# A level-embedding transformer tower on one core: ternary weights transposed by DMA, scores in plain fp32

## The chip, the core and the metric

The kernel runs on one core of a Trainium2 chip. The metric is the device time of one execution in microseconds. The kernel is written by hand: each of the engines TensorE (PE), VectorE (DVE), ScalarE (ACT), GpSimd (POOL) and SyncE (SP) runs its own list of instructions in order, and semaphores say what each waits for.

## What is computed

A table of 32 level embeddings is the only input of the attention, so `x` (16 sequences of 128 tokens) is turned into bracket levels first; after that the tower works on levels and counts, not on tokens. Cut to what matters:

```
delta  = is_open(x) - is_close(x);  levels = scan(clip(level + delta, 0, 31))
h      = level_emb[levels] * 0.15
h     += attention(layernorm(h))        # 16 query heads, 4 kv heads of 16, D = 256
Wq1, Wq2 = clip(round(W / (mean|W| + 1e-5)), -1, 1)       # ternary, W1 1024x256, W2 256x1024
h     += relu(layernorm(h) @ Wq1.T + b1) @ Wq2.T + b2     # output 16 x 128 x 256, fp32
```

## The kernel before

All tokens of a sequence that are at one level have one row, so there are 16 sequences x 32 levels = 512 rows, in four groups `g` of 128 rows (four sequences each). The stages are:

- **Head.** Constants by iota and comparison, the level scan on DVE, normalised table, queries and keys (`queries`, `keys`, `values`). Queries and keys are split in a high and a low fp32r part (`query_hi`, `query_lo`, `key_hi`, `key_lo`), and `scores_t(g)` adds for each group two fp32r matmuls of 512 columns and a bf16 one that masks absent levels (lines 1153, 1154, 1158). `less_max` subtracts the maxima, `exps(g)` takes the exponential on ACT.
- **Middle.** `context`, `inverse_sums`/`normalise` (`rec`, `cn`), `context_t`, `out_proj`, then `add_table`, `row_stats`, `row_moments`, `variance_eps` on DVE, the root on POOL (`inverse_root`, line 445), the normalised rows `xn2`, their transposes `rows_t` and their split in `xhi` (ACT) and `xlo` (DVE).
- **Weights, beside the middle.** `magnitudes` sums |W| on ACT in four passes of 128x1024 (line 528). W1 becomes ternary on ACT (`rounded`, line 537, and `ternary`, line 542), W2 on DVE (`signs`, line 867, and `ternary`, line 882). PE transposes both with an identity, `weights_t(u)`, u = 0 to 7, four 128x128 blocks each (line 1240), and ACT copies each result from PSUM (`weights_out(u)`, lines 549 and 551) to `w1T` or `w2T`.
- **FFN.** `ffn1(h, j)`: half `h` of the rows, hidden chunk `j`, four matmuls of 256 columns into PSUM bank `pswt` (line 1258); `hidden` on ACT applies the ReLU (`hr`, and `hh` for some), `hidden_lo` on DVE makes the low part; `ffn2(j, g)`: two matmuls of 256 columns into `psmisc` (line 1273). The order of both is written out by hand. Two `pswt` banks mean that an `ffn1` can start only when ACT has read the one before the last.
- **Tail.** `final(g)`, `spread(g)` (rows to tokens by one-hot matmuls, lines 1295 to 1298), `result(g)` copies to SBUF, ACT the first two sequences of a group and DVE the other two, and stores of 256 KB go out per pair.

Dependences that the change touches: `ffn1(0, j)` waits for `a_wt`, the copies of W1; `ffn2(j, 0)` waits for those of W2. POOL does four roots, two scaled means (`mr2`, for `norm_rows(2)` and `norm_rows(3)`) and four `residual`s behind its `counted_values`. Warm matmuls on zeros (`warm_up`, `keep_warm`) fill PE's gaps.

Of the kernel before, what the change touches and what calls it, by code (L numbers as in the profile page):

```python
# [36 lines left out]
def level_tower(nc, x, emb, Wq, bq, Wk, bk, Wv, bv, Wo, bo, W1, b1, W2, b2, out):  # L37
# [20 lines left out]
    with ctx:  # L58
# [35 lines left out]
        ident1 = sb("ident1", [P, P], BF16)  # L94
        ident2 = sb("ident2", [P, P], BF16)
# [52 lines left out]

        pmx = sb("pmx", [P, 2, P])
# [57 lines left out]
        c_ident = sem("c_ident")  # L207
# [51 lines left out]
        v_khi = sem("v_khi")  # L259
        v_klo = sem("v_klo")  # L260
        a_qhi = sem("a_qhi")
        v_qlo = sem("v_qlo")
# [3 lines left out]
        p_s = sem("p_s")  # L266
        v_pmx = sem("v_pmx")
# [26 lines left out]
        v_sgn = sem("v_sgn")  # L294
        p_gam = [sem(f"p_gam{i}") for i in range(2)]
        v_thr = sem("v_thr")
        v_tern = sem("v_tern")
        p_wt = sem("p_wt")
        a_wt = sem("a_wt")
# [18 lines left out]

        SPREAD_IN_PARTS = (0, 1)
# [13 lines left out]
        w1_rows = W1.rearrange("(p j) d -> p j d", j=FC)  # L333
# [10 lines left out]
        def _(sp):  # L344
# [4 lines left out]
            sp.dma_start(bvr[:], bv.unsqueeze(0)).then_inc(d_bv, 16)  # L349
            sp.dma_start(bkc[:], bk.unsqueeze(0).unsqueeze(2).to_broadcast([2, KVD, 1])).then_inc(d_bk, 16)  # L350
# [24 lines left out]
        def _(pool):  # L375
# [99 lines left out]
            counted_values(3)  # L475
            inverse_root(0)
            inverse_root(1)
            inverse_root(2)
            inverse_root(3)
            scaled_mean(2)  # L480
            scaled_mean(3)
            residual(0)
            residual(1)
            residual(2)
# [3 lines left out]
        def _(act):  # L488
            act.dma_start(tok3[:], x.unsqueeze(0).to_broadcast([3, B, S])).then_inc(d_tok, 16)
            act.dma_start(bq2[:], bq.rearrange("(k a e d) -> a e k d", k=KV, a=2, e=2)).then_inc(d_bq, 16)  # L490

# [20 lines left out]
            def query_hi(i):  # L512
                act.wait_ge(p_q, 1)
                c = slice(64 * i, 64 * i + 64)
                nc.scalar.activation(qs[c, :].rearrange("p (a e l) -> p a e l", a=2, e=2)[:, :, i, :],
                                     psg[3][c, 0:2 * L].rearrange("p (a l) -> p a l", a=2), ACT.Copy).then_inc(a_qhi, 1)
# [9 lines left out]
            def magnitudes(w, i):  # L526
                act.wait_ge((d_w1, d_w2)[w][i], 16)
                nc.scalar.activation(aw[:, w, i * 1024:(i + 1) * 1024], halves(w, i), ACT.Abs,  # L528
                                     accum_out=asum[:, 2 * w + i:2 * w + i + 1]).then_inc(a_abs, 1)

            def rounded(q):
                act.wait_ge(a_abs, 2)
                act.wait_ge(v_inv, 1)
                act.wait_ge(c_magic, 2)
                c = slice(1024 * q, 1024 * q + 1024)
                src = w1[:].rearrange("p j d -> p (j d)")[:, c]
                nc.scalar.activation(aw[:, 0, c], src, ACT.Identity, bias=magic[:, 0:1], scale=inv[:, 0:1]).then_inc(a_rnd, 1)
# [521 lines left out]
        def _(pe):  # L1059
# [157 lines left out]
            def weights_t(u):  # L1217
                w, i = divmod(u, 4)
                if w == 0:
# [4 lines left out]
                    if u == 1:  # L1224
                        pe.wait_ge(v_thr, 1)
# [200 lines left out]
```

## Time and profile before

| | us |
|---|---|
| three runs | 55.86, 55.99, 53.93 (median 55.86) |
| profiled execution | 54.04 |
| its span, first to last instruction | 52.0 |
| PE busy in it | 45.6 (88%) |
| DVE, ACT, POOL busy | 38.0 (73%), 34.2 (66%), 15.7 (30%) |

The chain of work that ended last is 76% PE, 10% DVE, 3% POOL and 1% ACT. The largest shares of it are the ffn1 matmuls with 16% and the ffn2 matmuls with 15%. A plain fp32 matmul stands in the trace as two records. The time of an execution is about 2 us longer than its span. In a timeline a row starts with its start and its busy time, then engine, line, operation, tiles and number.

### The profile page before, as it was taken

How to read it: one execution, taken by the hardware profiler on the slowest of the kernel's cores; microseconds unless marked ns; L12 is line 12 of the kernel's file. 1: busy time of each engine (PE TensorE's matmuls, PEld its weight loads, DVE VectorE, ACT ScalarE, POOL GpSimd, SP SyncE). 2: the span in 40 equal slices, each digit the busy share in tenths (PEclk: the TensorE clock that was granted, in tenths of full speed). 3: DMA queues.
4: the chain of work that ended last, by engine and by line, in shares of the span. 5: the costliest groups of instructions: out<-in, count | busy, mean ns of one | idle time of the engine just before them, and what ended most of it. 6: DMA issues, size and time to landing. Idle time of an engine off the chain costs nothing.

```text
span 52.0 us, 1206 instructions
## 1 busy us (share of the span) xinstructions
PE 45.6 (88%) x394; PEld 36.3 (70%) x394; DVE 38.0 (73%) x141; ACT 34.2 (66%) x77; POOL 15.7 (30%) x37
## 2 busy tenths in 40 slices
PE   0999999999999799999999999999999999993000
PEld 0336469894758688768679999989999798860000
DVE  3558994698985289999999996269858889659100
ACT  0083231380799997989988999999967793509000
POOL 5689952000005950009200579970000000000000
PEclk9999999999999999999999999999999999999997
DMA  0183919999753100000000000000000005555893
GB/s 0 36 234 77 44 63 350 410 432 368 198 124 98 47 7 0 0 0 0 0 0 13 0 0 0 0 6 0 0 0 0 0 13 200 203 208 195 295 385 127
DMA packets 4658, 5.37 MB, mean 103 GB/s; under 512 B 1117, under 2 KB 4141, under 8 KB 4653
## 3 DMA queue, kind: packets, MB, share of 16 engines
q1 hardware_dynamic: 4312, 5.02, 31.2%
q10 hardware_dynamic: 341, 0.29, 1.6%
q8 instruction: 3, 0.05, 0.4%
q14 instruction: 2, 0.02, 0.1%
HBM read 3.21 MB, written 2.10 MB: 102 GB/s over the span
## 4 chain that ended last, share of the span: by engine, by line
PE 76%; DVE 10%; POOL 3%; issue 1%; ACT 1%; DVEq 1%
PE pswt L1258 16%; PE psmisc L1273 15%; PE psg L1067 8%; PE psg L1063 5%; PE psg L1194 4%; POOL rs L445 3%; PE psg L1240 3%; DVE aw L952 2%; PE psg L1106 2%; PE psg L1153 2%; PE psg L1203 2%; PE psg L1154 2%; PE psg L1158 2%; DVE cn L892 2%; DVE hq L906 2%; DVE st L910 2%
## 5 line engine op out<-in xcount | busy, mean ns | idle before, releaser
L587 ACT ACTIVATE hr<-pswt,b1c 128x256 f32<-128x256 f32 x16 | 7.6, 484 | 1.2 <-PE pswt L1258 0.9
L1273 PE MATMUL psmisc<-w2T,hh 128*128 128x256 f32 x32 | 8.2, 285 | 0.0
L1273 PE MATMUL psmisc<-w2T,hl 128*128 128x256 f32 x32 | 8.1, 281 | 0.0
L937 DVE TENSOR_TENSOR hl<-hr,hh 128x256 fp32r<-128x256 f32 x16 | 6.7, 435 | 1.2 <-ACT hh L589 0.9
L1258 PE MATMUL pswt<-xhi,w1T 128*128 128x256 f32 x32 | 7.0, 299 | 0.0
L1258 PE MATMUL pswt<-xlo,w1T 128*128 128x256 f32 x32 | 6.4, 280 | 0.0
L1273 PEld LDWEIGHTS psmisc<-w2T,hh 128*128 128x128 f32 x32 | 6.0, 189 | 0.1
L1273 PEld LDWEIGHTS psmisc<-w2T,hl 128*128 128x128 f32 x32 | 6.0, 189 | 0.0
L445 POOL TENSOR_TENSOR rs<-ve,mhalf 128x1 f32<-128x1 f32 x4 | 2.7, 686 | 9.1 <-DVE ve L918 9.1
L440 POOL TENSOR_TENSOR voc<-vo,cpos 128x272 f32<-128x272 f32 x4 | 2.7, 714 | 8.1 <-DVE cpos L858 8.1
L1258 PEld LDWEIGHTS pswt<-xhi,w1T 128*128 128x128 f32 x32 | 4.9, 189 | 0.3
L1258 PEld LDWEIGHTS pswt<-xlo,w1T 128*128 128x128 f32 x32 | 4.9, 188 | 0.0
L1067 PE MATMUL psg<-warm 128*128 128x256 bf16 x24 | 4.7, 352 | 0.0
L528 ACT ACTIVATE aw<-w 128x1024 f32<-128x1024 f32 x4 | 4.2, 1055 | 0.0
L1194 PE MATMUL psg<-wo,cT 128*128 128x256 f32 x16 | 4.2, 394 | 0.0
L594 ACT ACTIVATE aw<-psg 128x256 f32<-128x256 f32 x6 | 2.0, 381 | 2.9 <-PE psg L1298 1.6
L1067 PEld LDWEIGHTS psg<-warm 128*128 128x128 bf16 x24 | 2.8, 126 | 1.5 <-issue 0.8
L1063 PE MATMUL psg<-warm 128*128 128x512 bf16 x6 | 2.7, 630 | 1.2 <-DVE tiny L666 1.2
L589 ACT ACTIVATE hh<-pswt,b1c 128x256 fp32r<-128x256 f32 x7 | 3.4, 482 | 0.0
L502 ACT ACT_TABLE_LOAD x1 | 1.3, 1283 | 2.8 <-issue 2.8
L1194 PEld LDWEIGHTS psg<-wo,cT 128*128 128x128 f32 x16 | 2.8, 190 | 0.3
L455 POOL TENSOR_TENSOR hb<-hq,b_bc 128x256 f32<-128x256 f32 x4 | 3.0, 782 | 0.0
(177 smaller groups left out, 108.4 us busy)
## 6 DMA issues: line engine op xcount, KB each, us to landing
w<-in_L_ffn_W_dram SPq DMA_DIRECT2D x4, 512.0 KB, 6.8
out_dram<-aw SPq DMA_DIRECT2D x7, 256.0 KB, 2.4
wq<-in_L_attn_Wq_dram SPq DMA_DIRECT2D x1, 256.0 KB, 3.5
wo<-in_L_attn_Wo_dram SPq DMA_DIRECT2D x4, 64.0 KB
out_dram<-aw ACTq DMA_DIRECT2D x1, 256.0 KB, 2.9
emb<-in_L_tok_level_emb_dram SPq DMA_DIRECT2D x1, 128.0 KB
bo_bc<-in_L_attn_bo_dram SPq DMA_DIRECT2D x1, 128.0 KB, 8.8
b_bc<-in_L_ffn_b_dram SPq DMA_DIRECT2D x1, 128.0 KB, 7.3
```

The source lines that it names most:

```text
L440: nc.gpsimd.tensor_tensor(voc[:, bs, :], vo[:].unsqueeze(1).to_broadcast([P, BG, VW]), cpos[:, bs].unsqueeze(2).to_broadcast([P, BG, VW]), ...
L445: nc.gpsimd.tensor_tensor(rs2[:, g:g + 1], ve2[:, g:g + 1], mhalf[:], ALU.pow).then_inc(g_rs2, 1)
L455: nc.gpsimd.tensor_tensor(hb[:, g, :], hq[:, g, :], b2_bc[:], ALU.add).then_inc(g_hb, 1)
L528: nc.scalar.activation(aw[:, w, i * 1024:(i + 1) * 1024], halves(w, i), ACT.Abs, accum_out=asum[:, 2 * w + i:2 * w + i + 1]).then_inc(a_ab ...
L587: nc.scalar.activation(hr[:, n % NHR, :], pswt[n % 2][:, 0:RH], ACT.Relu, bias=b1c[:, j:j + 1]).then_inc(a_hr, 1)
L589: nc.scalar.activation(hh[:, n, :], pswt[n % 2][:, 0:RH], ACT.Relu, bias=b1c[:, j:j + 1]).then_inc(a_hh, 1)
L937: V.tensor_tensor(hl[:, n, :], hr[:, n % NHR, :], hh[:, n, :].bitcast(F32), ALU.subtract).then_inc(v_hl, 1)
L1063: mm(bank[:, :], warm[:, 0:P], warm[:], start=True, stop=True)
L1067: mm(bank[:, 0:256], warm[:, 0:P], warm[:, 0:256], start=True, stop=True)
L1194: ins = mm(psg[g][:, 0:D], cT[:, g, e].rearrange("p b l -> p (b l)"), wo[:, e, :], start=(e == 0), stop=(e == H2 - 1))
L1258: ins = mm(pswt[n % 2][:, 0:RH], w1T[:, j, k, :], part[:, k, HALF * h:HALF * (h + 1), :].rearrange("p g n -> p (g n)"), start=(m == 0 and ...
L1273: ins = mm(psmisc[r][:, 0:D], part[:, n, r * P:(r + 1) * P], w2T[:, j, :], start=(j == 0 and m == 0), stop=(j == FC - 1 and m == 1))
```

## The change

- **Weights.** `weights_t` and `weights_out` are gone. Both matrices are rounded and signed on ACT (`rounded(w, i)`, `ternary(w, i)`, halves of 128x1024). SP then transposes each half with one `dma_start_transpose` (256 KB of bf16) from SBUF to SBUF, and POOL casts it to fp32r with two `weights_in(u)` of 128x512. W2's magnitudes are summed on DVE by a reduction with absolute value. `signs` and DVE's `ternary` go. W1 is loaded with row `j*128 + p` on partition `p`, `b1` likewise.
- **Scores.** Queries (64 rows) and keys stay plain fp32, stored twice, on partitions 0 to 63 and 64 to 127. `scores_t` is one fp32 matmul of 64 rows per group for groups 0 to 2. `masks` adds all four masks, each from 32 rows. Group 3 (`SUBTRACTED`) gets no score matmul; `score_table` makes the 128x128 table once, ACT copies it to `st`, and `arguments(3)` adds it on DVE before the exponential. The selection matmuls of `less_max` are as before.
- **Loads.** The biases `bv` and `bk` go from SP's queue to ACT's, the tokens come in three DMAs.
- **Order.** All lists are reordered: POOL's constants, DVE's constants, PE's `queries` ahead of `keys`, the FFN lists, `keep_warm` counts. The level scan runs on 128 partitions.
- **Results.** ACT copies sequences 0 and 2 of a group and DVE 1 and 3, so that each pair needs one copy of each. The dummy exponential (`table_load`) moves behind `result(0)`.

The core of the diff:

```diff
-        w1_rows = W1.rearrange("(p j) d -> p j d", j=FC)
+        w1_rows = W1.rearrange("(j p) d -> p j d", p=P)
@@ sync
-            sp.dma_start(bvr[:], bv.unsqueeze(0)).then_inc(d_bv, 16)
-            sp.dma_start(bkc[:], bk.unsqueeze(0).unsqueeze(2).to_broadcast([2, KVD, 1])).then_inc(d_bk, 16)
...
-            sp.dma_start(b1c[:], b1.rearrange("(p j) -> p j", j=FC)).then_inc(d_b1, 16)
+            sp.dma_start(b1c[:], b1.rearrange("(j p) -> p j", p=P), allow_slow_non_contiguous=True).then_inc(d_b1, 16)
...
+            for w in range(2):
+                for i in range(2):
+                    sp.wait_ge(a_tern, 2 * w + i + 1)
+                    sp.dma_start_transpose(wT[:, w, FC * i:FC * i + FC, :], tern[:, w, 1024 * i:1024 * i + 1024]).then_inc(d_wt[2 * w + i], 16)
...
@@ gpsimd
+            def weights_in(u):
+                w, q = divmod(u, FC // 2)
+                pool.wait_ge(d_wt[u // 2], 16)
+                src = wT[:, w, 4 * q:4 * q + 4, :].rearrange("p (j k) f -> p j k f", k=KC)
+                if w == 0:
+                    nc.gpsimd.tensor_copy(w1T[:, 2 * q:2 * q + 2], src).then_inc(g_wt, 1)
+                else:
+                    nc.gpsimd.tensor_copy(w2T[:, 2 * q:2 * q + 2, :].rearrange("p j (k f) -> p j k f", k=KC), src).then_inc(g_wt, 1)
...
@@ scalar
-            act.dma_start(tok3[:], x.unsqueeze(0).to_broadcast([3, B, S])).then_inc(d_tok, 16)
+            for i in range(3):
+                act.dma_start(tok3[B * i:B * i + B, :], x).then_inc(d_tok, 16)
...
+            def rounded(w, i):
+                if w == 0:
+                    act.wait_ge(a_abs, 2)
+                act.wait_ge(v_inv, w + 1)
...
+            def ternary(w, i):
+                act.wait_ge(a_rnd, 2 * w + i + 1)
+                c = slice(1024 * i, 1024 * i + 1024)
+                nc.scalar.activation(tern[:, w, c], aw[:, w, c], ACT.Sign, bias=magic[:, 1:2]).then_inc(a_tern, 1)
...
@@ vector
-            def signs(i):
+            def magnitudes(i):
                 dve.wait_ge(d_w2[i], 16)
-                V.tensor_scalar(sg[:, i * 1024:(i + 1) * 1024], w2[:, i, :], 0.0, 0.5, ALU.is_ge, ALU.subtract).then_inc(v_sgn, 1)
+                V.tensor_reduce(asum[:, 2 + i:3 + i], w2[:, i, :], AX_X, ALU.add, apply_absolute_value=True).then_inc(v_abs, 1)
...
+            def arguments(g):
+                dve.wait_ge(p_et, 1)
+                dve.wait_ge(a_st, 1)
+                V.tensor_tensor(et[:, g], st[:].unsqueeze(1).to_broadcast([P, BG, P]), psg[g][:, :].rearrange("p (b n) -> p b n", b=BG),
+                                ALU.add).then_inc(v_arg, 1)
...
@@ tensor
-            def scores_t(g):
-                rhs = qs[:].unsqueeze(1).to_broadcast([P, BG, P])
-                mm(psg[g][:, :], khi[:], rhs, start=True, stop=False)
-                mm(psg[g][:, :], klo[:], rhs, start=False, stop=False)
...
+            def score_table():
+                mm(psmisc[0][:, 256:256 + P], ktm[64:P, :], qs[64:P, :], start=True, stop=True).then_inc(p_st, 1)
+
+            def scores_t(*gs):
+                for g in gs:
+                    h = slice(64 * (g % 2), 64 * (g % 2) + 64)
+                    mm(psg[g][:, :], ktm[h, :], qs[h, :].unsqueeze(1).to_broadcast([64, BG, P]), start=True, stop=False, skip_group_check=True)
+
+            def masks():
+                pe.wait_ge(c_seln, 2)
+                pe.wait_ge(v_gone, 1)
+                for g in range(NG):
+                    q = slice(L * g, L * (g + 1))
+                    mm(psg[g][:, :], gone[q, :], seln[q, :].unsqueeze(2).to_broadcast([L, BG, P]), start=g in SUBTRACTED, stop=False,
+                       skip_group_check=True)
...
             def ffn1(h, j):
...
+                if h == 0 and j % 2 == 0:
+                    pe.wait_ge(g_wt, j // 2 + 1)
...
             def ffn2(j, g):
...
                 if g < HALF and j % 2 == 0:
-                    pe.wait_ge(a_wt, 5 + j // 2)
+                    pe.wait_ge(g_wt, 5 + j // 2)
```

On POOL, behind the counted values (`voc`), there stood before the four roots (`rs`), the two scaled means (`mr`) and the residuals (`hb`):

```order
L440 TENSOR_TENSOR voc<-vo,cpos 128x272 x4
L445 TENSOR_TENSOR rs<-ve,mhalf 128x1 x4
L449 TENSOR_SCALAR mr<-mv,rs 128x1 x2
L455 TENSOR_TENSOR hb<-hq,b_bc 128x256 x4
```

and now, in the same place, with the casts of the transposed weights (`w1T`, `w2T` from `wT`):

```order
L442 TENSOR_TENSOR voc<-vo,cpos 128x272 x4
L466 TENSOR_TENSOR hb<-hq,b_bc 128x256
L456 TENSOR_TENSOR rs<-ve,mhalf 128x1 x2
L450 CAST w1T<-wT 128x512 x2
L456 TENSOR_TENSOR rs<-ve,mhalf 128x1
L460 TENSOR_SCALAR mr<-mv,rs 128x1
L450 CAST w1T<-wT 128x512 x2
L452 CAST w2T<-wT 128x512
L456 TENSOR_TENSOR rs<-ve,mhalf 128x1
L460 TENSOR_SCALAR mr<-mv,rs 128x1
L452 CAST w2T<-wT 128x512
L466 TENSOR_TENSOR hb<-hq,b_bc 128x256
```

Eight casts moved in among the roots, and one residual ahead of them. On PE, from the third output projection to the first ffn2, there stood before (`L1240` is a weight transpose, `L1194` the output projection, `L1258` ffn1):

```order
L1194 MATMUL psg<-wo,cT 128x256 x2
L1185 MATMUL psg<-identf,cn 128x128 x2
L1203 MATMUL psg<-identf,xn 128x128 x4
L1240 MATMUL pswt<-ident,tern 128x128 x4
L1194 MATMUL psg<-wo,cT 128x256 x2
L1240 MATMUL pswt<-ident,tern 128x128 x4
L1240 MATMUL psg<-ident,tern 128x128 x8
L1258 MATMUL pswt<-xhi,w1T 128x256 x2
L1258 MATMUL pswt<-xlo,w1T 128x256 x2
```

and now (`L1197` output projection, `L1206` row transposes, `L1237` ffn1):

```order
L1197 MATMUL psg<-wo,cT 128x256 x2
L1062 MATMUL psmisc<-warm 128x256 x4
L1206 MATMUL psg<-identf,xn 128x128 x4
L1062 MATMUL psmisc<-warm 128x256 x3
L1197 MATMUL psg<-wo,cT 128x256 x2
L1237 MATMUL pswt<-xhi,w1T 128x256 x2
L1237 MATMUL pswt<-xlo,w1T 128x256 x2
L1237 MATMUL pswt<-xhi,w1T 128x256 x2
L1237 MATMUL pswt<-xlo,w1T 128x256 x2
L1206 MATMUL psg<-identf,xn 128x128 x2
```

Warm matmuls stand where transposes stood, and the rows of group 2 are transposed behind the second ffn1.

## Rows read from the trace of the kernel before

**Rows 1.** Busy time by stretch: PE, PEld, DVE, ACT, POOL, clock, DMA, GB/s.
```profile
23.00:28.00 5.00, 4.91 (x41) 3.90 (x42) 4.88 (x16) 4.62 (x11) 1.49 (x2) 1.00 0.00 0
...
34.00:41.00 7.00, 7.00 (x60) 6.86 (x58) 5.81 (x17) 5.95 (x16) 0.78 (x2) 1.00 0.00 1
```

**Rows 2.** Timeline of PE: start us, busy us, then the instruction.
```profile
15.74 0.67 PE L1166 MATMUL psg<-ms,sel 32*128 32x128 f32 x16
...
27.80 0.48 PE L1258 MATMUL pswt<-xhi,w1T 128*128 128x256 f32 x2
...
30.20 0.28 PE L1273 MATMUL psmisc<-w2T,hh 128*128 128x256 f32 x1
...
35.03 0.51 PE L1258 MATMUL pswt<-xhi,w1T 128*128 128x256 f32 x2
```

**Rows 3.** Timelines of ACT and DVE, the marks of head and middle.
```profile
16.83 1.56 ACT L565 ACTIVATE et<-psg 128x512 f32<-128x512 f32 x3
...
23.62 1.14 ACT L542 ACTIVATE tern<-aw,magic 128x1024 bf16<-128x1024 f32 x1
...
21.48 0.43 DVE L906 TENSOR_TENSOR hq<-psg,eb 128x256 f32<-128x256 f32 x1
...
23.31 0.10 DVE L918 TENSOR_SCALAR ve<-mv 128x1 f32<-128x1 f32 x1
...
26.67 0.74 DVE L926 TENSOR_TENSOR xlo<-psg,xhi 128x256 fp32r<-128x256 f32 x2
```

**Rows 4.** The chain that ended last: start us, us, what.
```profile
3.92 1.71 PE psg L1067 x8
...
7.35 0.76 PE psg L1067 x6
...
13.24 0.23 PE psg L1153
...
26.14 0.92 PE psg L1194 x4
...
28.99 0.31 PE psg L1240 x4
```

**Rows 5.** Groups of instructions by form: busy us, mean ns, then idle before.
```profile
L528 ACT ACTIVATE aw<-w 128x1024 f32<-128x1024 f32 x4 | 4.2, 1055 | 0.0
...
L882 DVE SCALAR_TENSOR_TENSOR tern<-aw,thr,sg 128x512 bf16<-128x512 f32 x4 | 2.9, 746 | 0.0
...
L537 ACT ACTIVATE aw<-w,magic,inv 128x1024 f32<-128x1024 f32 x2 | 2.5, 1253 | 0.0
...
L549 ACT ACTIVATE w1T<-pswt 128x512 fp32r<-128x512 f32 x4 | 2.4, 606 | 0.2 <-PE pswt L1240 0.2
...
L867 DVE TENSOR_SCALAR sg<-w 128x1024 bf16<-128x1024 f32 x2 | 1.4, 684 | 0.0
```

**Rows 6.** Timeline of PE, the spread of group 2 in plain fp32.
```profile
46.01 0.71 PE L1298 MATMUL psg<-fin,oh 32*128 32x256 f32 x8
```

**Rows 7.** DMAs: token issue, then landing of stores, of W1/W2, of `wq`.
```profile
0.73 1.33 ACTq L489 DMA_DIRECT2D tok<-in_x_dram  x1
...
DMA to landing us min/median/max: 2.1/2.5/3.2
...
DMA to landing us min/median/max: 5.6/6.8/8.0
...
wq<-in_L_attn_Wq_dram SPq DMA_DIRECT2D x1, 256.0 KB, 3.5
```

**Rows 8.** Groups by form on POOL: the root, the copy, the selector.
```profile
L445 POOL TENSOR_TENSOR rs<-ve,mhalf 128x1 f32<-128x1 f32 x4 | 2.7, 686 | 9.1 <-DVE ve L918 9.1
...
L432 POOL TENSOR_SCALAR sel<-jdx,pnum 128x512 fp32r<-128x512 int32 x1 | 2.0, 2007 | 0.0
...
L422 POOL COPY xT<-xT 128x256 f32<-128x256 f32 x1 | 0.4, 397 | 0.5 <-ACT xT L510 0.5
```

**Rows 9.** Busy time by stretch, the stores at the end.
```profile
50.00:51.00 1.00, 0.00 (x0) 0.00 (x0) 0.00 (x0) 0.00 (x0) 0.00 (x0) 1.00 1.09 386
```

More of the change, by code:

```diff
@@ L293, in level_tower @@
         a_abs = sem("a_abs")
-        v_sgn = sem("v_sgn")
+        v_abs = sem("v_abs")
         p_gam = [sem(f"p_gam{i}") for i in range(2)]
         v_thr = sem("v_thr")
-        v_tern = sem("v_tern")
-        p_wt = sem("p_wt")
-        a_wt = sem("a_wt")
+        d_wt = [sem(f"d_wt_{i}") for i in range(4)]
+        g_wt = sem("g_wt")
         p_f1 = sem("p_f1")
@@ L591, in result @@
             def result(g):
[L592 removed]
+                for b in range(0, BG, 2):
                     act.wait_ge(p_out, g * BG + b + 1)
[L594 to L595 removed]
+                    nc.scalar.activation(osb[:, g, b, :], out_banks(g)[b][:, 0:D], ACT.Copy).then_inc(a_out, 1)
+            query_weights(0)
+            query_weights(1)
+            rows_out()
             key_weights()
[L599 to L605 removed]
+            magnitudes(0)
+            query_out(0)
+            query_out(1)
+            table_out()
+            magnitudes(1)
             prefix_out()
[L607 removed]
             max_hi()
[L609 to L610 removed]
             exps(0)
@@ L613, in _ @@
             exps(2)
-            rounded(0)
+            exps(3)
+            rounded(0, 0)
             ctx_out(0)
             ctx_out(1)
-            exps(3)
-            rounded(1)
-            ternary(0)
+            ternary(0, 0)
+            rounded(0, 1)
             ctx_out(2)
-            ternary(1)
-            weights_out(0)
+            ternary(0, 1)
+            rounded(1, 0)
             ctx_out(3)
+            ternary(1, 0)
             x_hi(0)
-            weights_out(1)
             x_hi(1)
-            weights_out(2)
-            weights_out(3)
-            weights_out(4)
+            rounded(1, 1)
+            norm_rows(2)
             hidden(0, 0)
             hidden(0, 1)
-            weights_out(5)
+            ternary(1, 1)
             hidden(0, 2)
             hidden(0, 3)
+            norm_rows(3)
             hidden(0, 4)
-            norm_rows(2)
+            x_hi(2)
             hidden(0, 5)
-            norm_rows(3)
-            weights_out(6)
-            x_hi(2)
             x_hi(3)
@@ L669, in _ @@
             V.memset(drop[:], 0.0).then_inc(v_zero, 1)
-            V.memset(gone[:], 0.0).then_inc(v_zero, 1)
             dve.wait_ge(c_opc, 2)
@@ L986, in _ @@
             top_onehot()
-            signs(0)
             level_onehot(0)
             level_onehot(1)
+            count_blocks()
             max_parts()
-            count_blocks()
             counts_out()
-            signs(1)
+            magnitudes(0)
+            arguments(3)
             threshold(0)
@@ L1367, in _ @@
             ffn2(4, 0)
+            ffn2(5, 0)
             ffn1(1, 1)
-            ffn2(5, 0)
             ffn1(1, 2)
```

407 lines of the change are left out of this document (171 added, 236 removed).

## Prediction

> **What bounds the kernel now.** I read the windows first [rows 1]: TensorE (PE) is busy 4.91 of 5.00 us in 23 to 28 and all of 34 to 41, so in the second half every matmul is time. In 23 to 28 ScalarE (ACT, 4.62) and VectorE (DVE, 4.88) are nearly as full. The timeline of PE [rows 2] gives the marks that I carry through the sum: `less_max` starts at 15.74, the first ffn1 matmul at 27.80, the first ffn2 at 30.20, `ffn1(1, 0)` (first of the second half of the tokens) at 35.03. Behind PE's last matmuls only copies and stores are left to the end at 52.0. The ACT and DVE timelines [rows 3] show what decides the front: the exponentials start at 16.83, behind the fourth magnitude pass on ACT, though `less_max` is about done at 16.4; the second half of ternary W1 is ready at 24.76; the first variance at 23.4; the second `x_lo` of the pair ends at 27.41. So the rows are there 0.4 before `ffn1(0, 0)` at 27.80; PE is still at weight transposes.
>
> **What the change removes.** Thirty-two bf16 transposes leave PE (eight groups of four, at most the 0.31 of the group shown [rows 4], so up to 2.5 us) and eight ScalarE evacuations of 0.61 leave ACT, 4.9 us [rows 5]. DVE loses four `tern` operations (0.746) and two `sg` (0.684), 4.35 us. The fp32r split of keys and queries goes, with its high and low passes: before, each group of scores is three 512-column matmuls, each 0.23 in the chain [rows 4], 2.8 us in all.
>
> **What it adds.** W2's magnitudes move from ACT (two of 1.055, 2.1 us) to DVE as two reductions of 1024 columns. No row has one. Bounds are 0.68 (`sg`, the same columns) and 1.5 (twice the 512-column `tern`) [rows 5]; I take 1.2, one column per cycle as the slope from 0.43 at 256 columns (`add_table` [rows 3]) suggests. W2's rounding and sign are now ACT's: two of 1.253 and two of 1.14, 4.8 us. ACT as a whole is then 4.9 + 2.1 - 4.8 = 2.2 us lighter. DVE gets 2.4 for the reductions and 0.7 for `arguments(3)` (512 columns from PSUM, by 0.43 for 256).
>
> Plain fp32 scores: `out_proj` is such a matmul at 256 columns, 0.92 in the chain for a pair [rows 4], so 0.47 each; so 0.9 for 512 columns. The spreads in plain fp32 with 32 rows [rows 6] take 0.71 for four of 256 columns where 0.47 each would be 1.9, so matmuls on different rows of the array overlap. `scores_t(0, 1)` uses rows 0 to 63 and 64 to 127 and I cost the pair at 0.9; if they don't overlap it is 1.8. The four masks, 32 rows each, cost 0.25 together instead of 0.92.
>
> Transposes by DMA: four of 256 KB. No row has one. Nearest are the stores of the same 256 KB (2.1 to 3.2 to landing, median 2.5) and the load of `wq`, also 256 KB, 3.5 [rows 7]. Bounds: 2.1, and 8.0, the slowest load of W1/W2. I take 3.0, between store and load: the queue is idle then. TensorE pays 0.31 for four such blocks [rows 4]. The Trainium skill (VectorE: DVE Perf Modes, "The three transpose paths") gives 390 ns for it, 1309 ns for a 128x128 block through the DMA crossbar, and advises TensorE. Eight blocks one after the other would by it be 10.5 us, an estimate from that page, and no row here shows it.
>
> Casts on GpSimd (POOL): eight of 128x512 bf16 to fp32r. Nearest are COPY of 256 columns at 0.397, so 0.72 to 0.8 for 512, and the integer TENSOR_SCALAR of 512 columns at 2.007 [rows 8]. It is a copy, so I take 0.75; both ends stay in the range.
>
> **The sum, step by step.** *Loads.* SP sheds two small issues ahead of W1, so W1 comes earlier. ACT issues three token loads for one and two biases more; at half the 1.33 of the broadcast one [rows 7] that is 2 us more ahead of its first copies, which then end at about 6.1, needed at 7.3. The tokens come 0.3 later at most, `drops` wait for 6.5. `b1c` in 4-byte pieces is wanted at 28, `b2_bc` behind it at 21.5, issued by 12. All of it is covered; without cover the ACT issues would cost those 2 us.
>
> *Head.* The first levels come later (12 instead of 8 warm matmuls, 0.214 each [rows 4], before `drops`), but queries run before keys. PE reaches `scores` at 11.6, by the order of its rows. Then `scores_t(2)` 0.9, prefix transposes at 12.85, the pair 0.9, maxima at 14.1, `ms` at 15.3, `less_max` from 15.4 (15.74 before) to 16.05. The exponentials then start at once, since ACT holds no magnitudes: 16.05 for 16.83, 0.8 earlier. `exps(3)` waits for `arguments(3)`, ready at 17.4 (reduction 15.5 to 16.7, addition 0.7), which is before ACT is free at 17.6.
>
> *Middle.* `cn(0)` starts at 18.0. The second reduction stands ahead of `add_table(0)` on DVE and eats part: 21.05 for 21.48. With `threshold(1)` in between, the first variance is at 23.15. POOL's roots take 0.75 each [rows 8], `norm_rows` follow at 24.0 and 24.75, with `rows_t` at 24.45 and 25.2. On ACT: ternary W1 ready at 21.05 and 23.5, rounding of W2 waits for the threshold (23.1), ternary W2 first half ready at 26.0, then `x_hi(0)`, `x_hi(1)` to 26.6. `x_lo(1)` ends at 27.05 and `ffn1(0, 0)` starts there: 0.75 earlier. The transposes that filled PE there are gone.
>
> *Weights.* Transpose 0 is issued at 21.05 and lands at 24.05. POOL is busy with two roots until 24.7, then casts 0 and 1 to 26.2: 0.85 of slack to the first ffn1. Root and mean of group 2 (1.3) to 27.6; casts 2, 3, 4 to 29.85, if transpose 2 (26.05) lands by 29.1, which is exactly at 3.0. So the first ffn2 starts at 29.9 (30.20 before), behind four ffn1 (to 29.65; ACT's `rounded(1, 1)` and `norm_rows(2)` delay `hidden(0, 0)` and so `ffn1(0, 2)` to 28.65). Behind cast 4 on POOL stand root and mean 3, which `norm_rows(3)` and the second half's rows wait for: they end at 31.1, cast 5 at 31.9, `residual(1)` at 32.65, cast 6 at 33.45 (transpose 3 issued at 30.1 behind `hidden(0, 1)`, lands at 33.1, slack 0). PE: ffn2(2) at 32.05 behind `rows_t(3)`, which waits for `norm_rows(3)`; `ffn1(0, 7)` at 33.3, `ffn2(4, 1)` at 33.8, `ffn1(1, 0)` at 34.05 for 35.03: 1.0 earlier. On both sides the same eight ffn2 and eight ffn1 are done then, and the rest has the same matmuls and stays PE's.
>
> *Tail.* Copies alternate between ACT and DVE, so the first pair of group 2 goes to the queue after one copy each and not two: 0.2 earlier. The last 1 MB runs at up to 386 GB/s [rows 9], and there the start counts: 0.15. Sum: 54.04 (the profiled execution; its span is 52.0) - 1.0 - 0.15 = 52.9. The median shown is 55.86, the fastest run 53.93: the profiled execution belongs to the fast end, and I forecast at that end and count 2% (about what a measurement of this kernel tells from no change) from it: faster below 52.96, slower above 55.12. Against the median the same shift would be 54.7.
>
> **Rivals.** *W2's transposed weights a little late (0.27).* A transpose of 4.0, or casts of 1.0, puts cast 4 at 30.8; the first ffn2 at 30.9, cast 5 at 32.9, cast 6 at 34.9, `ffn1(1, 0)` at 35.2: 54.0. For it: slack 0 at two places of the sum. Against: the stores, 2.5. Halfway (3.5) is 53.4.
> *Clearly late, slower (0.18).* The DMA transpose is the bound: from 4.0 up each us to landing puts cast 6, and behind it `ffn2(4, 1)` and all of the second half, 1 us later; it decides against the change at 5.1 (55.1); at 6.0 it gives 56.0. If the queue also works off one at a time, T each: landings at 21.05 + 4T, so at T = 6 the last comes at 45 and the time is 65. That the blocks of an instruction go serially has 0.04 of the 0.18. The Trainium skill's figure (VectorE: DVE Perf Modes, "The three transpose paths") stands at that end: by it the last lands at 63 and the time would be 83, an estimate from that page. Casts at the 2.007 of the integer row give cast 6 at 42 and 61 us. For lateness: W1's and W2's loads took 5.6 to 8.0; against: those queued behind others [rows 7].
> *PE's clock falls (0.04).* PE is now sparse from 21 to 27, by my sum some 3.5 us of matmuls in 6, with ten warm matmuls less dense than the 32 transposes were. Up to 7 us a 256-column warm matmul takes 0.21, after it 0.127 [rows 4], the two levels of 1.2 and 2.4 GHz: half the clock for the first 3 us of ffn would cost 1.5 and give 54.4. The granted clock is 1.00 in both windows of [rows 1].
> *The front gives nothing (0.05).* If the two score matmuls don't overlap, maxima come at 15.0 and `less_max` at 16.2, the exponentials at 16.9: 0.8 lost again, half of it hidden behind the transposes; 53.4.
>
> **How the numbers follow.** Forecast as summed 0.46, with a range of its own of 52.3 (transposes as fast as the stores) to 53.3; 0.40 of it is faster, 0.06 the same. Same beside it: the first rival (0.27), the last (0.05) and half of the third (0.02), together 0.40. Slower: 0.18 and the other half of the third, 0.20. The range goes from 52.2 to 55.9, leaving out the serial queue and the slow casts above it (some 0.08 of the chance) and transposes faster than the stores below it (0.05).
>
> **What would show it.** Right: exponentials at about 16.1; `x_lo(1)` at 27; DMA_TRANSPOSE to landing about 3; CAST on POOL about 0.75; first ffn2 at 29.9; `ffn1(1, 0)` at 34; no wait of PE on POOL above 0.3. Wrong: PE waiting for `w2T`'s cast by more than 1 us, casts waiting for DMA, 0.21 per 256 columns anywhere after 8 us, or two score matmuls of 0.9 end to end.

## The result and the profile after

The changed kernel takes 59.76 us in the median of four executions (59.0 to 60.77), the kernel before 54.89 beside it (53.26 to 55.99). The ratio is 1.107, with a 95% interval of 1.086 to 1.129: slower by 10.7%. The forecast of 52.9 and its range to 55.9 missed it. Some executions of nearly every kernel here, that before too, run longer than the rest, so each ratio compares only those within 1.5% of the fastest of their kernel, and the medians given are of all.

| | before | after |
|---|---|---|
| profiled execution, us | 54.04 | 60.77 |
| its span | 52.0 | 58.7 |
| PE busy | 45.6 (88%) | 47.3 (80%) |
| DVE, ACT, POOL busy | 38.0, 34.2, 15.7 | 39.9, 32.3, 19.6 |

The page of the changed kernel, first its engines over 40 equal slices of the span (1.47 us each) and the granted clock in tenths. PE's row dips to 5, 0, 0 and 2 from the eighth slice on; the clock's row falls to 5 in the ninth and stays there for seven slices:

```profile
PE   1999999500299999999999599999999999999000
DVE  3859994000573805989799989998998998687500
PEclk9999999955555559999999999999999999999965
```

The waits of the same execution (us in total, times, longest) name the place:

```profile
DVE ktm L818 <- DMA bkc<-in_L_attn_bk_dram: 5.8, 1, 5.8
...
PE psmisc L1131 <- DVE ktm L818: 4.7, 1, 4.7
```

`ktm` adds the key bias `bk` to the keys. That bias now comes by the last load on ACT's queue: its row in the timeline of ACT's DMA issues, then the chain that ended last (start us, us, what), in which one load is 11.45 us of 58.7:

```profile
3.75 0.56 ACTq L512 DMA_DIRECT2D bkc<-in_L_attn_bk_dram  x1
```

```profile
3.75 11.45 DMA bkc<-in_L_attn_bk_dram
```

DVE starts `ktm` at 15.33, PE the first score matmul at 15.73 after 4.67 us without work. What TensorE's clock did in that time stands in the windows (busy time of PE, PEld, DVE, ACT, POOL, then clock, DMA share, GB/s):

```profile
5.00:11.00 6.00, 6.00 (x47) 4.60 (x45) 4.35 (x15) 3.34 (x9) 3.19 (x7) 1.00 0.93 320
11.00:12.00 1.00, 0.06 (x1) 0.00 (x0) 0.00 (x0) 0.00 (x0) 0.00 (x0) 0.95 0.27 101
12.00:22.00 10.00, 6.26 (x17) 2.70 (x18) 3.59 (x17) 1.70 (x4) 0.00 (x0) 0.50 0.28 72
```

PE was full up to 11 us, idle from 11.06, and the clock went from 2.4 to 1.2 GHz behind that. The whole score stage, from 15.73 to about 22, ran at the lower level. The marks of the forecast, in the timelines of PE and ACT: exponentials at 23.85 where [rows 3] have 16.83, first ffn1 at 34.73 and `ffn1(1, 0)` at 41.58 where [rows 2] have 27.80 and 35.03.

```profile
19.11 2.08 PE L1153 MATMUL psg<-qs,ktm 64*128 64x512 f32 x4
...
34.73 0.48 PE L1237 MATMUL pswt<-xhi,w1T 128*128 128x256 f32 x2
...
41.58 0.40 PE L1237 MATMUL pswt<-xhi,w1T 128*128 128x256 f32 x2
```

```profile
23.85 1.58 ACT L592 ACTIVATE et<-psg 128x512 f32<-128x512 f32 x3 [1.22 <-PE psg L1169]
```

From the exponentials to the end it is 34.85 us, where the forecast had 34.8 (50.85 less 16.05) and the kernel before 35.17. So the whole miss of 7.8 us lies ahead of the exponentials. The theory after this result: `bk` is 128 pieces of 4 bytes, now on ACT's queue beside the 2 MB of W1 and W2 on SP's. It crawls through shared DMA engines, and the idle TensorE behind it loses its clock. Rivals: the loss comes from another part of the change and `bk` only marks it, the place in ACT's own queue is to blame, or the clock falls by itself.

### The profile page after: what moved, and what is told of

Read it like the earlier page. It is cut to its first block, busy times and chain, and to the rows that moved or that the text cites. A ratio compares the mean times of both kernels' runs of the same rounds, so it can differ in the third digit from the quotient of the medians.

```text
span 58.7 us, 1173 instructions
## 1 busy us (share of the span) xinstructions
PE 47.3 (80%) x376; PEld 35.7 (61%) x376; DVE 39.9 (68%) x135; ACT 32.3 (55%) x70; POOL 19.6 (33%) x45
## 3 DMA queue, kind: packets, MB, share of 16 engines
q1 hardware_dynamic: 10068, 6.07, 34.2%
HBM read 3.21 MB, written 2.10 MB: 90 GB/s over the span
## 4 chain that ended last, share of the span: by engine, by line
PE 30%; ACT 25%; DMA 19%; DVE 9%; ACTq 5%; issue 3%; DVEq 1%
DMA bkc<-in_L_attn_bk_dram 19%; PE psmisc L1252 10%; ACT tern L573 7%; PE psg L1153 6%; PE pswt L1237 6%; ACT aw L563 4%; ACT aw L566 3%; ACT hr L614 3%; ACTq L509 2%; ACTq L510 2%; PE psmisc L1144 2%; DVE asum L871 2%; DVE aw L954 2%; ACT xn L600 2%; ACT hh L616 2%
## 5 line engine op out<-in xcount | busy, mean ns | idle before, releaser
L1252 PE MATMUL psmisc<-w2T,hh 128*128 128x256 f32 x32 | 8.9, 300 | 0.1
L939 DVE TENSOR_TENSOR hl<-hr,hh 128x256 fp32r<-128x256 f32 x16 | 8.1, 525 | 0.6 <-ACT hh L616 0.2
L1237 PE MATMUL pswt<-xhi,w1T 128*128 128x256 f32 x32 | 6.6, 288 | 0.0
L1237 PE MATMUL pswt<-xlo,w1T 128*128 128x256 f32 x32 | 6.4, 282 | 0.0
L1237 PEld LDWEIGHTS pswt<-xhi,w1T 128*128 128x128 f32 x32 | 4.9, 189 | 0.6 <-issue 0.4
L1237 PEld LDWEIGHTS pswt<-xlo,w1T 128*128 128x128 f32 x32 | 4.9, 188 | 0.0
L573 ACT ACTIVATE tern<-aw,magic 128x1024 bf16<-128x1024 f32 x4 | 4.7, 1166 | 0.0
L1131 PE MATMUL psmisc<-ktm,qs 64*128 64x128 f32 x2 | 0.8, 496 | 4.7 <-DVE ktm L818 4.7
L1197 PE MATMUL psg<-wo,cT 128*128 128x256 f32 x16 | 4.2, 386 | 0.0
L1153 PE MATMUL psg<-qs,ktm 64*128 64x512 f32 x6 | 4.0, 1111 | 0.0
```

What stands on the lines that cost most here:

```text
L573: nc.scalar.activation(tern[:, w, c], aw[:, w, c], ACT.Sign, bias=magic[:, 1:2]).then_inc(a_tern, 1)
L939: V.tensor_tensor(hl[:, n, :], hr[:, n % NHR, :], hh[:, n, :].bitcast(F32), ALU.subtract).then_inc(v_hl, 1)
L1153: mm(psg[g][:, :], ktm[h, :], qs[h, :].unsqueeze(1).to_broadcast([64, BG, P]), start=True, stop=False, skip_group_check=True)
L1197: ins = mm(psg[g][:, 0:D], cT[:, g, e].rearrange("p b l -> p (b l)"), wo[:, e, :], start=(e == 0), stop=(e == H2 - 1))
L1237: ins = mm(pswt[n % 2][:, 0:RH], w1T[:, j, k, :], part[:, k, HALF * h:HALF * (h + 1), :].rearrange("p g n -> p (g n)"), start=(m == 0 and ...
L1252: ins = mm(psmisc[r][:, 0:D], part[:, n, r * P:(r + 1) * P], w2T[:, j, :], start=(j == 0 and m == 0), stop=(j == FC - 1 and m == 1))
```

## Experiments

### The key bias back where it was, and alone where it went

The changed kernel with only this edit (`e1_bk_sp`):

```diff
@@ sync, between Wv and W1
+            sp.dma_start(bkc[:], bk.unsqueeze(0).unsqueeze(2).to_broadcast([2, KVD, 1])).then_inc(d_bk, 16)
@@ scalar, last load
-            act.dma_start(bkc[:], bk.unsqueeze(0).unsqueeze(2).to_broadcast([2, KVD, 1])).then_inc(d_bk, 16)
```

> The changed kernel with the load of bk alone back on SP's queue, between Wv and W1 (bv stays on ACT's). Both theories of the late bk (T1: its 4-byte pieces take turns with the pieces of W1/W2 of the other queue; T2: ACT's queue is slow by itself for it) expect bk to land by about 7 us, keys' scale-and-mask on VectorE right behind the key matmuls (11 us), no idle TensorE before the scores and a full clock from 8 us on: 51 us of span, 53.0 us, so 0.97 of before. If bk is only one of several faults, the time stays above 54.5.

Measured: 53.77 in the median of ten (lowest 52.71), before 53.62, ratio 0.992, interval 0.987 to 0.997. The one line takes away all of the 10.7%; below the kernel before it comes by 0.8%, where I had forecast 3%. The profiled execution shows `ktm` waiting for PE's keys and no longer for a DMA (its clock fell without an idle TensorE, see the last section, so no other mark is read from it):

```profile
11.62 0.35 DVE L818 SCALAR_TENSOR_TENSOR ktm<-psmisc,bkc,km 128x128 f32<-128x128 f32 x1 [1.85 <-PE psmisc L1088]
```

The reverse, the kernel before with only that load moved from SP to the end of ACT's queue (`e2_before_bk_act`):

```diff
@@ sync
-            sp.dma_start(bkc[:], bk.unsqueeze(0).unsqueeze(2).to_broadcast([2, KVD, 1])).then_inc(d_bk, 16)
@@ scalar, behind bq
+            act.dma_start(bkc[:], bk.unsqueeze(0).unsqueeze(2).to_broadcast([2, KVD, 1])).then_inc(d_bk, 16)
```

> The kernel before with this one load moved to the end of ACT's queue and nothing else. T1 and T2: the wait of VectorE for bk appears here too, 10 to 12 us from issue (2.8) to landing, at about 13 to 14, scores at 14.5 for 11.2; with 3 us idle TensorE may lose its clock: +3.5 without, +6 with it: 57.5 to 60 us. If the rest of the change makes the wait, this kernel stays at before's time.

Measured: 58.89 (58.23 to 60.77), ratio 1.095, interval 1.082 to 1.108. The wait for `bk` and its load in the chain are those of the changed kernel, without any other part of it. The load was issued at 2.82, before the first load of the weights (3.21), and was late all the same:

```profile
DVE ktm L797 <- DMA bkc<-in_L_attn_bk_dram: 4.7, 1, 4.7
...
2.82 10.41 DMA bkc<-in_L_attn_bk_dram
```

Both directions agree, so the move of one 512-byte load is the cause, and the rival of another part falls.

### Why it lands late

First place on ACT's queue instead of the last (`e3_bk_act_first`), to part the place in the queue from the queue:

```diff
@@ scalar
+            act.dma_start(bkc[:], bk.unsqueeze(0).unsqueeze(2).to_broadcast([2, KVD, 1])).then_inc(d_bk, 16)
             for i in range(3):
                 act.dma_start(tok3[...
```

> The changed kernel with bk on ACT's queue still, but as its first DMA (0.7 us), ahead of the tokens. T1: it is through before W1 moves (from 5 us) and lands in about 2 to 3.5 us; 53 to 53.5 us. T2 (queue slow by itself): 11 us again, landing at 12, scores at 12.5; 54.5 to 57 us.

Measured: 61.3 (60.82 to 62.46), ratio 1.147, interval 1.135 to 1.159, which neither theory gave. `bk` itself was in time now, but what stands behind it on the queue was not. DVE waited 2.7 for the tokens (0.7 in the changed kernel), and `bq`, issued at 3.27, is the load in the chain, with 6.08:

```profile
DVE opened L759 <- DMA tok<-in_x_dram: 2.7, 1, 2.7
...
3.27 6.08 DMA bq<-in_L_attn_bq_dram
...
9.49 0.66 PE L1094 MATMUL psg<-two,bq 2*128 2x64 f32 x2 [0.91 <-DMA bq<-in_L_attn_bq_dram]
```

The rows give two reasons without any hold-up in the queue. The issue of `bk` takes 1.15 of ACT's time, so the tokens are issued from 1.92 on and not from 0.73. And `bq`, whose outermost dimension is 2 as well, is now issued behind the first load of W1 (2.75) and not ahead of it, so it meets the same traffic as `bk` did. Whether the pieces of `bk` also hold up their own queue is not shown. PE sat idle for both loads; the clock's row is below full from the sixth slice to the seventeenth and the exponentials come at 25.52.

Same place as in the change, but SP issues W1 and W2 only when `bk` has landed (`e5_w_waits_bk`):

```diff
@@ sync
+            sp.wait_ge(d_bk, 16)
             for i in range(2):
                 c = slice(i * FC // 2, (i + 1) * FC // 2)
                 sp.dma_start(w1...
```

> The changed kernel, bk last on ACT's queue as there, but SP issues W1 and W2 only after bk has landed. T1 (bk takes turns with W's pieces): without W on the move bk lands within 3 us of its issue at 3.8, so by 7; W1 is 4 us later (issued at 7 for 2.7), its magnitudes at 12 and the rest with it, so 53.5 to 56 us; the wait of VectorE for bk is gone. T2 (queue slow by itself): bk lands at 15 again and W1 after it, over 62 us.

Measured in one execution: 57.1 beside 54.07. The load still stands last on ACT's queue, issued at 3.73. SP waited 3.9 for it and issued W1 at 6.57, so it had landed at most 2.84 after its issue, where it took 11.45 before. `ktm` starts at 10.05, waiting 0.84 for PE and nothing for a DMA:

```profile
SPq L350 <- DMA bkc<-in_L_attn_bk_dram: 3.9, 1, 3.9
...
6.57 0.93 SPq L350 DMA_DIRECT2D w<-in_L_ffn_W_dram  x2
...
10.05 0.35 DVE L819 SCALAR_TENSOR_TENSOR ktm<-psmisc,bkc,km 128x128 f32<-128x128 f32 x1 [0.84 <-PE psmisc L1089]
...
ACT aw L554 <- DMA w<-in_L_ffn_W_dram: 3.2, 1, 3.2
```

The weights are now the late ones (ACT waits 3.2 for them), and the clock's row has four slices at 5 from the tenth on, so the total tells nothing of `bk`. The packets agree with the landing. In the window from 5 to 11 us, queue 10 (ACT's) moved 94 packets in the changed kernel and 44 more from 11 to 15.2; with W held back it moved 130 in the first of them, all before 7 us, while SP's queue (q1) stood still. First the changed kernel in its two windows, then this one (its q1 packets all come behind 7 us):

```profile
q1 hardware_dynamic: 1311, 1.92, 92.1%
q10 hardware_dynamic: 94, 0.00, 0.8%
...
q1 hardware_dynamic: 1204, 0.51, 45.2%
q10 hardware_dynamic: 44, 0.00, 0.6%
```

```profile
q1 hardware_dynamic: 1062, 1.08, 57.4%
q10 hardware_dynamic: 130, 0.00, 1.0%
```

(Columns: packets, MB, share of 16 engines.) The crawl needs the traffic of SP's queue beside it. That agrees with what the Trainium skill says in "DMA: Bandwidth & Descriptors", section "Queues, rings and completion order": each DMA engine takes turns between the queues it has work for, a packet at a time. The trace doesn't show single engines' turns, so that part stays a statement of the Trainium skill. The bulk load pays too: the slowest of the four loads of W1 and W2 took 9.7 to land in the changed kernel, 8.0 in the kernel before.

The same load as two DMAs whose outermost dimension is the 64 values, again last on ACT's queue and with W not held back (`e6_bk_wide`, and timed as `e9_bk_wide_timed`):

```diff
-            act.dma_start(bkc[:], bk.unsqueeze(0).unsqueeze(2).to_broadcast([2, KVD, 1])).then_inc(d_bk, 16)
+            for r in range(2):
+                act.dma_start(bkc[KVD * r:KVD * r + KVD, :], bk.unsqueeze(1)).then_inc(d_bk, 16)
@@ vector
-                dve.wait_ge(d_bk, 16)
+                dve.wait_ge(d_bk, 32)
```

> The changed kernel, bk last on ACT's queue, same 4-byte pieces and same number of them, but as two DMAs whose outer dimension is the 64 values and not the 2 copies, so that they spread over more DMA engines. T1 in the form that one engine's pieces wait in a row: with 64 in a row 11 us, with 4 to 8 in a row 1 to 2 us: landing at 6 to 8, 53 us. If any 4-byte pieces beside W are slow however spread: 11 us again, 59.5 us.

> The kernel with bk in two wide transfers at the end of ScalarE's queue, now timed. The one look gave 53.9 beside 54.07. The contention theory says that with bk in time nothing else of the change costs anything, so ratio 0.985 to 1.0; a rival, that the loss of the changed kernel is only hidden by a lucky execution, would put it above 1.02.

Measured: 53.9 in one execution beside 54.07, then 53.49 in the median of ten beside 53.8, ratio 1.002, interval 0.997 to 1.007. The same pieces on the same queue at the same moment land in 6.4 (median of the two, the row of DMA issues) instead of 11.45, and the clock falls in neither of the two profiled executions:

```profile
bkc<-in_L_attn_bk_dram ACTq DMA_DIRECT2D x2, 0.2 KB, 6.4
...
11.11 0.35 DVE L819 SCALAR_TENSOR_TENSOR ktm<-psmisc,bkc,km 128x128 f32<-128x128 f32 x1 [1.62 <-DMA bkc<-in_L_attn_bk_dram]
```

`bk` is not fully in time here: the second of the two loads lands at 10.97, `ktm` still waits 1.62 for it and PE 0.34 for `ktm`. What differs is the outermost dimension, 2 before and 64 now, and that there are two loads; two loads with a narrow outermost dimension were not run, so the two are not parted. By the Trainium skill ("DMA: Bandwidth & Descriptors", section "Why a DMA increments its semaphore by 16 and not by 1", under "How many engines (k)") that dimension limits over how many DMA engines a load is spread, by its rule at most 2 before and 16 now. The landing moved the way of that rule, though less than eightfold, and it came later than the 6 to 8 that I had expected: beside W even a spread load of small pieces took 6.4.

### What the clock adds to the wait

The changed kernel with 37 warm matmuls (`keep_warm(37, psg[0])` between `values()` and `scores()`), which fill PE while it waits for `bk` (`e4_fill_pe`):

> The changed kernel with 37 more warm matmuls of 256 columns (0.12 each, 4.5 us) ahead of the scores, in the wait for bk. bk lands as late as before, at about 15. If the wait alone costs (clock irrelevant): same time as the changed kernel, 59.5. If the idle time also takes the clock down, as the changed kernel's rows show (0.50 of full speed for 10 us): the stretch from the scores to the exponentials shrinks from 8.1 to about 4.5 us, 56.0 us.

Measured: 57.41 (57.09 to 60.6), ratio 1.075, interval 1.063 to 1.087. That is between the 59.5 of a wait alone and the 56.0 of my sum for the clock. The wait for `bk` is still there, the fall of the clock isn't, and the pair of score matmuls takes 1.13 in place of 2.08:

```profile
PEclk9999999999999999999999999999999999999975
...
14.68 0.35 DVE L818 SCALAR_TENSOR_TENSOR ktm<-psmisc,bkc,km 128x128 f32<-128x128 f32 x1 [5.12 <-DMA bkc<-in_L_attn_bk_dram]
...
16.96 1.13 PE L1153 MATMUL psg<-qs,ktm 64*128 64x512 f32 x4
...
20.27 1.58 ACT L592 ACTIVATE et<-psg 128x512 f32<-128x512 f32 x3 [1.22 <-PE psg L1169]
```

With `e9_bk_wide_timed`, whose exponentials start at 16.68, the 7.8 us of the miss in the profiled execution fall into three. From `ktm` to the exponentials it is 8.52 in the changed kernel, 5.59 here and 5.57 in e9. So the clock costs 8.52 less 5.57, 2.95. `ktm` itself comes at 15.33 for 11.11, 4.22. The remaining 0.63 is e9's 16.68 against the forecast's 16.05. The sum is 7.80. The profiled execution of the changed kernel is its longest, and the shares by the ratios are smaller: from 1.107 to 1.075 (e4) is 1.7 us for the clock, and from 1.075 to 1.002 (e9) 3.9 us for the wait.

That the clock falls by itself is not enough as a rival. In all 13 recorded executions of the three kernels with a late load (changed, e2, e3) the mean granted clock is 0.926 or less. It is 0.938 or less in 10 of the 56 of e1, e4 and e7 to e11, and 0.973 or more in the others.

### What the rest of the change is worth

The edit of `e1_bk_sp` and, besides, the fourth group of scores on PE too (`e7_four_on_pe`): no subtraction, no table, masks ahead of the maxima.

```diff
-            score_table()
-            scores_t(2)
+            scores_t(2, 3)
@@
-            keep_warm(4, psg[3])
```

> The changed kernel with bk back on SP's queue as in the run before this one with bk alone moved back, and besides with the fourth group's scores on TensorE too: scores_t(2, 3) as a second pair on rows 0 to 63 and 64 to 127, no subtraction on VectorE, no argument table, the masks ahead of the maxima. If the head term of the prediction was mis-sized by the path table, group 2's scores, warm matmuls and maxima, the exponentials start at 16.1 to 16.4 (16.93 with bk repaired alone) and the time is 0.5 to 0.8 us under that kernel: 52.9 to 53.3 beside 53.6, ratio 0.98 to 0.99. If the head is bound by what comes before the scores (levels, keys, queries), the exponentials stay at 16.8 to 17.0 and the ratio at 0.992.

Measured: 53.85 in the median of ten (lowest 52.78), before 53.8, ratio 0.992, interval 0.984 to 1.000. That is what `bk` alone gave, and the exponentials start at 17.14 in its profiled execution, later than either theory had them. So subtracting one group on VectorE neither costs nor brings anything measurable. The head is bound by another chain. PE did the pair at 13.51 to 14.6 and then waited 0.81 for `ms`, which waited for ACT's copy of the maxima:

```profile
16.43 0.67 PE L1166 MATMUL psg<-ms,sel 32*128 32x128 f32 x16 [0.81 <-DVE ms L866]
...
16.02 0.35 DVE L866 SCALAR_TENSOR_TENSOR ms<-mhi,lowrow,psmisc 128x128 fp32r<-128x128 f32 x1 [1.00 <-ACT mhi L549]
```

That kernel with PE's head in the order and with the warm matmuls of the kernel before (`e8_head_order`, and again with more executions as `e11_both_again`), and this order on top of `e1_bk_sp` alone (`e10_order_alone`):

```diff
-            keep_warm(12, psg[0])
+            keep_warm(8, psg[0])
             drops()
-            keep_warm(1, psg[0])
+            keep_warm(5, psg[0])
             table_t()
-            keep_warm(2, psg[0])
+            keep_warm(6, psg[0])
+            keys()
             query_bias()
             queries()
-            keep_warm(3, psg[0])
+            keep_warm(5, psg[0])
             levels_out()
-            keep_warm(7, psg[0])
-            keys()
```

> The kernel with four score groups on TensorE (above), with TensorE's order and number of warm matmuls at the head as in the kernel before (8, 5 and 6, keys, bias, queries, 5). Theory A: the drop of the granted clock that three of ten executions of the kernel with bk alone moved back had comes from the sparser head order; then it is gone here and every execution lies within 1.5% of the fastest. Theory B: the order has nothing to do with it, and some execution is again at about 57 to 59. The time of the others: 52.9 to 53.5 by either.

> The kernel of e8_head_order again with more rounds, since its interval [0.970, 0.992] from four executions leaves open whether it beats both kernels by more than bk alone moved back (0.992). If it does, the interval ends below 0.987; if it was scatter, the ratio is 0.985 to 0.997.

> The changed kernel with bk on SP's queue and with the head's order and warm matmuls of the kernel before (8, 5, 6, keys, bias, queries, 5), all else as changed: fourth group subtracted on VectorE. It parts the two edits of e8_head_order. If the head order carried that kernel's gain (0.981), this one comes out at 0.975 to 0.987; if the gain was the fourth group on TensorE or scatter of four executions, it stays at the 0.992 of bk alone moved back, 0.987 to 0.997.

Measured: e8 53.39 beside 53.8, ratio 0.981 (0.970 to 0.992, four executions); e11, the same kernel, 53.41 beside 53.51, 0.993 (0.988 to 0.997, twelve executions); e10 53.8 beside 53.51, 1.011 (1.005 to 1.016). The 0.981 was scatter for the most part. The order does not keep the clock up either: it fell in 1 of the 4 and in 2 of the 12 executions, so the theory that the sparser head order takes it down has no support. With `bk` repaired the best versions are 0.8% under the kernel before, and none beats it by more than 2%. The order alone came out above both of its forecasts. Each beside its own kernel before, it is 1.8% worse than the change's own order (1.011 for the 0.992 of e1, measured on different chips). Its profiled execution does not say why in the head: its exponentials start at 16.32, earlier than e9's 16.68. It shows one loss behind: the last transpose landed in 3.5 where the others took 2.7 or 2.8, POOL waited 1.57 for it and PE 0.46 for POOL:

```profile
33.55 1.48 POOL L453 CAST w2T<-wT 128x512 fp32r<-128x512 bf16 x2 [1.57 <-DMA wT<-tern]
...
34.42 0.36 PE L1252 MATMUL psmisc<-w2T,hh 128*128 128x256 f32 x1 [0.46 <-POOL w2T L453]
```

That is the forecast's rival of late W2 in one execution, and e5's is a second (3.7 to landing, PE waiting 0.5). Whether it explains e10's ratio is open, since one execution was profiled.

## Why the prediction was wrong

**The step that failed.** It is the paragraph *Loads*: "ACT issues three token loads for one and two biases more; at half the 1.33 of the broadcast one [rows 7] that is 2 us more ahead of its first copies", and then "All of it is covered". It priced the issues of the moved loads and where they put ACT's copies, and never asked when `bk` lands on its new queue nor who waits for it. The same paragraph had W1 come earlier, and it did, at 2.68 for 4.21, which is ahead of the issue of `bk` at 3.75. The issue of `bk` ended at about 4.3, and the runs with it in time start `ktm` at 10 to 11; I took the 6 us between as cover without a row for the landing. The rows to doubt it were there: W's landings of 5.6 to 8.0 [rows 7] say how full the DMA engines are in just that stretch, and the diff says that the load is 128 pieces of 4 bytes. With e5, e6 and e9 the price is known: 11.45 from issue to landing beside W, at most 2.84 with W held back, 6.4 beside W as two loads with an outermost dimension of 64. In time it is on SP's queue ahead of W.

**The clock.** The third rival named the right mechanism and the wrong place: it looked for sparse PE work from 21 to 27 and gave it 0.04. The clock fell at 12, behind the idle stretch that the late load made, and cost 2.95 in the profiled execution, 1.7 by the ratios (e4 against the changed kernel). From 21 to 27 the forecast that it most likely holds was right: in e9 it does.

**Head.** With `bk` spread (e9) the exponentials start at 16.68 for the 16.05 forecast and the 16.83 before. The term was mis-sized by 0.63. The maxima start at 14.43 for 14.1, 0.33 late, since the prefix transposes stand at 13.00 for 12.85 and the fp32 pair takes 1.13 and not 0.9. It is not the 0.34 that PE still waits for `ktm` there, since `scores` starts at 11.52 for the 11.6 of the sum. `ms` makes up 0.07 (15.56 for 15.3). `less_max` starts at 15.96 for 15.4: `ms` lasts 0.35, and the sum had left 0.1 for it. The other 0.07 is `less_max` itself. Overlap of the two fp32 matmuls on rows 0 to 63 and 64 to 127 was right: the pair takes 1.13, one group alone 1.02, so the single group was mis-sized by 0.12 too.

**Middle.** Right. From the exponentials to the first ffn1 it is 10.88 for 11.0 forecast. The DVE reduction took 1.21 for 1.2.

**Weights.** Right in the changed kernel. DMA_TRANSPOSE to landing was 2.7 to 2.8 for 3.0, so the serial blocks of the second rival did not come, and casts took 0.61 for 0.75. The casts did wait for the DMA, 1.3 in two places, which the prediction had named as a sign of being wrong; here it was hidden, since PE waited for no cast. The rival of slightly late transposes came in e5 and e10 only, as 0.5 of waiting on PE. Tile `wT` of the changed kernel:

```profile
L363 SPq DMA_TRANSPOSE wT<-tern x4: 1232/1283/1338, 28.7 to 37.5; - x4
L450 POOL CAST w1T<-wT x4: 609/612/672, 32.3 to 35.3; 128x512 fp32r<-128x512 bf16 x4
...
DMA to landing us min/median/max: 2.7/2.7/2.8
```

From the exponentials to `ffn1(1, 0)` it is 17.73, where the forecast had 18.0 and the kernel before 18.20.

**Tail.** Half right. From the last spread to the end of the span e9 needs 5.87 (45.73 to 51.6) for 5.99 before, so 0.12 of the 0.15 forecast. But from `ffn1(1, 0)` to that spread it is 11.32 (34.41 to 45.73), and before it was 10.98: "the rest has the same matmuls and stays PE's" was wrong by 0.34. The rows of e9:

```profile
16.68 1.58 ACT L593 ACTIVATE et<-psg 128x512 f32<-128x512 f32 x3 [1.22 <-PE psg L1170]
...
34.41 0.40 PE L1238 MATMUL pswt<-xhi,w1T 128*128 128x256 f32 x2
...
45.73 0.71 PE L1277 MATMUL psg<-fin,oh 32*128 32x256 f32 x8
```

Its chain does not run over PE ahead of that stretch. From 18.13 to 33.54 it is all ACT (the rounding and signs of both matrices, with exponential, copies and ReLUs between them), then DVE's low parts, and the low part of `hidden` is what the ffn2 behind `ffn1(1, 0)` waits for:

```profile
33.26 0.28 ACT xhi L605
...
33.57 0.42 DVE xlo L929
...
34.52 0.85 DVE hl L940
35.38 0.04 issue
35.42 0.50 PE psmisc L1253 x2
```

In PE's timeline the matmuls of this stretch follow each other every 0.12 us, but between those at 35.01 and 35.42 it is 0.41: 0.29 of the 0.34. So PE starts the second half earlier and finds ACT and DVE not ready; that ACT was lighter as a whole did not help, since its work on the weights stood in the way of the rows. The `hl` at 34.52 also took twice its usual 0.43, and POOL was at a residual at that moment (34.30 to 35.95). Over the whole kernel the mean `hl` grew with the casts on POOL, before and in the changed kernel:

```profile
L937 DVE TENSOR_TENSOR hl<-hr,hh 128x256 fp32r<-128x256 f32 x16 | 6.7, 435 | 1.2 <-ACT hh L589 0.9
...
L939 DVE TENSOR_TENSOR hl<-hr,hh 128x256 fp32r<-128x256 f32 x16 | 8.1, 525 | 0.6 <-ACT hh L616 0.2
```

That POOL's work slows DVE's is suggested by this and was not tested; the sum had no term for it.

**The sum of the rest.** In the profiled executions e9's span is 51.6 for 52.0 before, where the forecast had 50.85. The missing 0.75 is, but for 0.05, 0.63 of the head and 0.34 of the second half, less the 0.27 by which the stretch from the exponentials to `ffn1(1, 0)` beat its forecast. The remaining gain of 0.4 does not show in the timed executions (1.002), where the forecast of 1.15 us less would be 0.979.

**What stays open.** How the DMA engines share out their turns one by one, how much of e9's gain is the spread and how much the split in two loads, whether POOL slows DVE, why e10 is slower, and why some executions lose clock without an idle TensorE.

## What to carry to other kernels

A load moved to another queue has three prices: its issue, what then waits behind it, and its landing beside the traffic of that moment. Cost the third for the smallest loads first: a few hundred bytes in 4-byte pieces can be the longest transfer of the kernel, so put them ahead of the bulk loads on the same queue (issued 0.4 us ahead on the other queue `bk` was still late in e2), or try an outermost dimension that spreads them. When a wait opens an idle stretch on TensorE, add what the lower clock costs the stage behind it; here that was 2.95 us on 4.22 us of wait in the profiled execution.

## What the runs showed of the hardware

- 128 pieces of 4 bytes, with an outermost dimension of 2, took 11.45 and 10.41 us beside 2 MB of weights on the other queue; as two loads with an outermost dimension of 64 they took 6.4; with the weights held back at most 2.84. `bq`, also with an outermost dimension of 2, took 6.08 when issued behind the first load of the weights.
- The granted clock fell from 2.4 to 1.2 GHz behind an idle stretch that began at 11.06 (0.95 in 11 to 12, 0.50 in 12 to 22), and did not fall in three of four executions where warm matmuls filled the same stretch. In `e1_bk_sp`'s profiled execution it fell without an idle stretch (0.59 in 9 to 10, then 0.50), with PE busy all the time; the window's row:

```profile
9.00:10.00 1.00, 1.00 (x9) 0.63 (x7) 0.74 (x6) 1.00 (x3) 0.00 (x0) 0.59 1.05 369
```

- A DMA transpose of 256 KB of bf16 from SBUF to SBUF landed in 2.7 to 2.8 us, except for one in e5 (3.7) and one in e10 (3.5), and took 1.23 to 1.34 of SP's issue time (in e7 up to 1.52, in e10 up to 2.17). A cast of 128x512 from bf16 to fp32r on GpSimd took 0.61, no more than ScalarE's evacuation from PSUM of the same shape [rows 5].
- Two plain fp32 matmuls of 512 columns on 64 rows each overlap: 1.13 for both at 2.4 GHz, 2.08 at 1.2.
